# A fused attention and mixture-of-experts kernel: the experts' tokens transposed one tile earlier, and GpSimd's queue reordered

## What is computed

```python
x = x + _L0_xattn_ref(ctx_1024, _layernorm(x), mask, ...)   # perceiver attention, 8 heads of 64, a final layer norm
x = x + _L0_ffn_ref(_layernorm(x), weight_q, weight_scale, bias)   # tokens quantised to int8, one 128x128 product
x = x + _L1_xattn_ref(_layernorm(x), ctx_1024, We, W2)      # attention over 77 context rows, softmax over the tokens
x = x + _L1_ffn_ref(_layernorm(x), Wr, br, W1, b1, W2, b2)  # 8 experts, top 1
# the last one, per token:
expert_idx = argmax(xf @ Wr.T + br)
h = relu(xf @ W1[e].T + b1[e]); y = h @ W2[e].T + b2[e]     # W1 512x128, W2 128x512, e = expert_idx
```

## Time and profile before

| | |
|---|---|
| median of 3 runs | 955.97 us (955.83 to 957.16) |
| the profiled execution | 956.35 us, span 954.6 us from the first to the last instruction |
| TensorE busy | 906.6 us (95%), its granted clock 0.998 of full speed |
| VectorE busy | 745.8 us (78%) |
| ScalarE busy | 693.6 us (73%) |
| GpSimd busy | 459.0 us (48%) |

### The profile page before, as it was taken

The page is one execution under the profiler, slowest core; times in us unless marked ns, Lnnn a source line. Parts: engine busy times, 40 slices in busy tenths (PEclk is TensorE's granted clock), DMA queues, the critical chain, the costliest instruction groups (busy, mean ns, idle before and its releaser), DMA issues.

```text
span 954.6 us, 30726 instructions
## 1 busy us (share of the span) xinstructions
PE 906.6 (95%) x11238; PEld 788.0 (83%) x11238; DVE 745.8 (78%) x2524; ACT 693.6 (73%) x1671; POOL 459.0 (48%) x1094
## 2 busy tenths in 40 slices
PE   3899999999999999999999999999999999899997
PEld 2688888788878887888888888888888878898997
DVE  4666788888878888888888888888888978877553
ACT  2777777777777777777777777777777766676664
POOL 4333333354545444544445454545453544777554
PEclk9999999999999999999999999999999999999999
DMA  6742000000000000000000000000000012245310
GB/s 177 222 131 43 2 2 2 3 13 3 10 5 11 5 8 7 8 8 8 7 8 8 8 8 7 8 8 8 7 8 7 8 41 72 65 96 108 96 52 21
DMA packets 45193, 31.44 MB, mean 33 GB/s; under 512 B 11555, under 2 KB 40166, under 8 KB 45046
## 3 DMA queue, kind: packets, MB, share of 16 engines
q1 hardware_dynamic: 39446, 19.93, 8.8%
q0 software_dynamic: 4320, 8.50, 2.8%
q10 hardware_dynamic: 1280, 1.05, 0.3%
HBM read 17.75 MB, written 12.17 MB: 31 GB/s over the span
## 4 chain that ended last, share of the span: by engine, by line
PE 68%; DVE 15%; ACT 8%; POOL 4%; issue 4%; DMA 0%; DVEq 0%; POOLq 0%; SPq 0%; ACTq 0%
PE ps L1652 9%; PE ps L1605 9%; PE ps L1580 7%; PE ps L1698 6%; PE ps L1396 5%; PE ps L1567 5%; PE ps L1559 5%; PE ps L1398 5%; PE ps L1397 5%; DVE sumsq L1292 4%; PE ps L1657 3%; PE ps L1682 2%; ACT probs L593 2%; ACT qk_hat L606 2%; PE ps L1435 1%
## 5 line engine op out<-in xcount | busy, mean ns | idle before, releaser
L1324 DVE TENSOR_TENSOR qk_hat<-ps,rstd 128x512 f32<-128x512 f32 x168 | 106.4, 685 | 50.1 <-POOL rstd L835 50.1
L1292 DVE TENSOR_REDUCE sumsq<-qk_hat 128x8 f32<-128x512 f32 x168 | 107.8, 678 | 34.6 <-ACT qk_hat L606 33.5
L828 POOL TENSOR_TENSOR rs_t<-rs_y 128x32 f32<-128x32 f32 x73 | 17.5, 240 | 234.7 <-ACT rs_y L647 234.7
L1605 PE MATMUL ps<-v_x,prob 128*64 128x65 f32 x2048 | 127.9, 225 | 2.1 <-ACT w_all L617 0.4
L1605 PE MATMUL ps<-v_c,prob 128*64 128x65 f32 x2048 | 124.3, 222 | 0.0
L1396 PE MATMUL ps<-w_hi,xc_hi 128*128 128x512 f32 x272 | 121.6, 447 | 2.3 <-POOL xc_lo L802 2.3
L666 ACT ACTIVATE prob<-ps,neg_shift 128x512 f32<-128x512 f32 x128 | 88.4, 691 | 48.6 <-PE ps L1652 48.6
L606 ACT ACTIVATE qk_hat<-ps 128x512 f32<-128x512 f32 x168 | 98.7, 599 | 33.5 <-PE ps L1398 27.9
L1605 PEld LDWEIGHTS ps<-v_x,prob 128*64 128x64 f32 x2048 | 105.0, 137 | 20.9 <-issue 19.3
L1652 PE MATMUL ps<-qT_all,kT_all 64*128 64x128 f32 x1536 | 111.6, 285 | 2.9 <-ACT w_all L617 1.2
L1398 PE MATMUL ps<-w_hi,xc_lo 128*128 128x512 f32 x272 | 108.0, 397 | 0.0
(11 more groups left out here) (241 smaller groups left out, 2248.2 us busy)
## 6 DMA issues: line engine op xcount, KB each, us to landing
x_res<-sorted_rows SPq DMA_DIRECT2D x71, 65.5 KB
w_all<-in_L_ffn_W_dram SPq DMA_DIRECT2D x16, 256.0 KB, 5.0
sorted_rows<-fill SPq DMA_DIRECT2D x8, 327.5 KB, 7.4
out_dram<-prob,x_res POOLq DMA_INDIRECT x71, 2.3
sorted_rows<-stage,idx POOLq DMA_INDIRECT x64, 2.4
ctx_res<-in_ctx_dram SPq DMA_DIRECT2D x8, 115.5 KB
x_res<-in_x_dram SPq DMA_DIRECT2D x1, 768.0 KB
sorted_rows<-fill SPq DMA_DIRECT2D x1, 524.0 KB, 4.7
```

What stands on the lines that cost most here:

```text
L1292: nc.vector.reduce_sum(sumsq[:, n * H:(n + 1) * H], sq[:, n * INNER:(n + 1) * INNER].rearrange("p (h d) -> p h d", d=DH), AX).then_inc(ss_ ...
L1324: nc.vector.tensor_tensor(qk_hat[:, n * INNER:(n + 1) * INNER].rearrange("p (h d) -> p h d", d=DH), ps_qk[:, n, :].rearrange("p (h d) -> p ...
L1605: last = nc.tensor.matmul(dst[half:half + DH, :], prob[:, kt, col + half:col + half + DH], v, start=kt == 0, stop=kt == 1)
```

## The change

- `turned(k)` names the tiles transposed in step k: tile 0 in step -1, tiles 1 and 2 in step 0, then tile k+2. TensorE, ScalarE (the copy) and VectorE (`t_now`, in `prep(k)` the tiles of `turned(k+1)`) follow it. TensorE waits before the transpose for the copy of tile n-2, and before the first products also for the relu of tile k-2.
- GpSimd, from round 64 on: variances, root and centred tokens first, then the bias, then two stores, the scatters, one store. The stores are those of one step earlier than before, so each round's last store goes to the next round. The last group's four scatters stand together after all of round 74's stores.
- The second table's four pieces go one to a step (steps 32 to 35), where steps 32 and 33 had two each.

```diff
+        def turned(k):
+            return [n for n in ({-1: [0], 0: [1, 2]}.get(k, [k + 2])) if 0 <= n < T]
 # ScalarE, tile(k)
-                if inside or has_tile(k + 1):
-                    past(act, "T_done", k + 4 * four + 1)
+                for n in [k + 2] if inside else turned(k):
+                    past(act, "T_done", n + 4 * four)
                     if k == -1:
                         act.wait_ge(lo_done, B)
-                    nc.scalar.activation(t_t[:, (k + 1) % 4, :], ps_t[(k + 1) % 2], ACT.Copy).then_inc(se["t_copied"], 1)
+                    nc.scalar.activation(t_t[:, n % 4, :], ps_t[n % 2], ACT.Copy).then_inc(se["t_copied"], 1)
...
-            at, turns = NA, (T - 1 - NA) // 4
+            at, turns = NA, (T - 2 - NA) // 4
 # GpSimd, run(j)
-                if rho == 2 and group(g, inside):
-                    after(pool, "x2_done", g - 1, inside)
-                    ...
-                if rho in (1, 2) and (inside or 0 <= g - 2 < NG - 1):
-                    scatter(g - 2, (2 * rho - 2, 2 * rho - 1), inside)
+                def biased():
+                    if rho == 2 and group(g, inside):
+                        after(pool, "x2_done", g - 1, inside)
+                        ...
+                def scattered():
+                    if rho in (1, 2) and (inside or 0 <= g - 2 < NG - 1):
+                        scatter(g - 2, (2 * rho - 2, 2 * rho - 1), inside)
+                if not tail(j, inside):
+                    biased()
+                    scattered()
...
                 if tail(j, inside):
+                    biased()
+                    store(tile_no(j, 0) - 1)
                     store(tile_no(j, 0))
+                    scattered()
                     store(tile_no(j, 1))
                     if g - 2 == NG - 1 and rho == 0:
                         pool.wait_ge(padded, 16 * E)
-                        scatter(g - 2, (0, 1), inside)
-                    store(tile_no(j, 2))
-                    if g - 2 == NG - 1 and rho == 0:
-                        scatter(g - 2, (2, 3), inside)
+                        scatter(g - 2, (0, 1, 2, 3), inside)
...
             rounds_written_out(run)
+            store(REST[0] - 1)
             for k in REST:
                 store(k)
 # VectorE, prep(k) and the steps after round 74
+                for n in turned(k + 1):
+                    past(dve, "T_done", n - 4)
+                    dve.wait_ge(ld[n % DEEP], 16 * (n // DEEP + 1))
+                    row = rows[:, n, :]
+                    nc.vector.tensor_scalar(t_now[:, n % 4, :], row[:, 0:D], row[:, D:D + 1], row[:, D + 1:D + 2],
+                                            ALU.subtract, ALU.mult).then_inc(se["t_set"], 1)
                 if has_tile(k + 2):
                     n, e = (k + 2) % 4, number[k + 2]
-                    past(dve, "T_done", k - 2)
-                    dve.wait_ge(ld[(k + 2) % DEEP], 16 * ((k + 2) // DEEP + 1))
                     row = rows[:, k + 2, :]
-                    nc.vector.tensor_scalar(t_now[:, n, :], ...).then_inc(se["t_set"], 1)
...
-                if k < REST[2]:
-                    for piece in (0, 1):
-                        last_table(2 * (k - REST[0]) + piece)
+                if k < REST[4]:
+                    last_table(k - REST[0])
                 finish(k)
 # TensorE, tile(k)
-                if has_tile(k + 1):
-                    past(pe, "t_set", k + 1)
-                    if k == 0:
+                for n in turned(k):
+                    past(pe, "t_set", n)
+                    past(pe, "t_copied", n - 2)
+                    if n == 1:
                         pe.wait_ge(exp_done, 4 * B)
-                    nc.tensor.transpose(ps_t[(k + 1) % 2], t_now[:, (k + 1) % 4, :], ident[:, :]).then_inc(se["T_done"], 1)
+                    nc.tensor.transpose(ps_t[n % 2], t_now[:, n % 4, :], ident[:, :]).then_inc(se["T_done"], 1)
                 if has_tile(k):
                     past(pe, "t_copied", k)
+                    past(pe, "relu_done", k - 2)
                     past(pe, "w1_set", k)
```

More of the change, by code:

```diff
@@ L769, in run @@
                     nc.gpsimd.tensor_copy(ctx_now[:, :, :], ctx_res[:, bass.ds(first, 3), :]).then_inc(s["ctx_taken"], 1)
-                if rho == 2 and group(g, inside):
-                    after(pool, "x2_done", g - 1, inside)
[L773 to L776, removed]
-                if rho in (1, 2) and (inside or 0 <= g - 2 < NG - 1):
-                    scatter(g - 2, (2 * rho - 2, 2 * rho - 1), inside)
+                def biased():
+                    if rho == 2 and group(g, inside):
+                        after(pool, "x2_done", g - 1, inside)
+                        pool.wait_ge(x1_done, G * (g + 1))
+                        nc.gpsimd.tensor_tensor(xb[:, :, :], grp(x_res, g),
+                                                bias_b[:, :].unsqueeze(1).to_broadcast([P, G, D]),
+                                                ALU.add).then_inc(s["xb2_done"], 1)
+                def scattered():
[4 more added lines that the diff above has]
+                    scattered()
                 def centred(j, g):
@@ L892, in prep @@
             def prep(k):
+                for n in turned(k + 1):
[4 more added lines that the diff above has]
+                                            ALU.subtract, ALU.mult).then_inc(se["t_set"], 1)
                 if has_tile(k + 2):
                     n, e = (k + 2) % 4, number[k + 2]
-                    past(dve, "T_done", k - 2)
-                    dve.wait_ge(ld[(k + 2) % DEEP], 16 * ((k + 2) // DEEP + 1))
                     row = rows[:, k + 2, :]
-                    nc.vector.tensor_scalar(t_now[:, n, :], row[:, 0:D], row[:, D:D + 1], row[:, D + 1:D + 2],
-                                            ALU.subtract, ALU.mult).then_inc(se["t_set"], 1)
                     past(dve, "relu_done", k - 2)
```

## The result

The changed kernel takes 957.9 us in the median of 14 runs (956.87 to 960.47), the kernel before 955.95 in 14 runs beside it (955.46 to 957.38). The ratio is 1.0021, 95% interval 1.0014 to 1.0028: some 1.95 us slower. The middle of the interval is just over the 0.2% named as the bound, and its lower end under it. The profiled execution took 958.9 us, its span is 957.2, the mean granted clock 0.996 (before 0.998). It is a late one among the 14; the fastest execution of each kernel differs by 1.4 us.

What follows compares the result with a forecast made beforehand. TensorE was taken as the bound, with GpSimd's chain binding from 810.51 to 834.15 us. Start +0.3, bias +0.2, parts 2 to 4 -0.2 sum to +0.3: 956.65 us profiled, 956.3 median, range 953.7 to 958.8.

Steps and rivals of the forecast that it cites:

- rival (b): Tile 41's load, behind fourteen stores and scatters ahead of the last scatter, comes late: 958.4 us; chance 0.17.
- Start, +0.3: Round 64: VectorE prepares tokens 1 and 2 in a row, one more 0.32 us operation TensorE waits for: +0.3 us.
- Waits for copies: TensorE's products no longer wait for ScalarE's token copies; TensorE 1.5 us ahead at round 68, -0.2 us after 840 us.
- The bias beside VectorE, +0.2: Group 14's bias, moved to about 795.2 us, runs beside VectorE's preparing of tile 5: +0.2 us, bounds 0 and 0.8.
- GpSimd's gap: GpSimd idle 2.35 instead of 0.70 us ahead of round 68's root; round 69's variances 1.65 us later, taken as +1.4.
- +0.95 at 839 us: Delay left at 839 us: +1.4 from GpSimd less 0.45, with VectorE's 0.40 us idle ahead of the logits' transpose regained.
- Late next, and no loss by itself: VectorE's sum of round 69, at 829.97 us, would wait for the bias done at 829.0 us, costing nothing by itself.
- Table, -1.5: One second-table piece a tile makes no tokens late and removes TensorE's 1.36 us hole: -1.5 us.
- Loads: Last scatter at 878.7, first load at 881.9 us; tile 41's load is later, so parts 2 to 4 give -0.2, not -0.75.
- rival (c): The table's spread doesn't help because VectorE loses its lead elsewhere; the 1.5 us stay: 957.5 us, chance 0.08.
- (a): Faster: GpSimd opens no gap, its root of 68 finds ScalarE free, or its chain is no bound: 953.8 us, chance 0.22.
- (d): Two-ahead copies don't free TensorE, since the wait on the relu of tile k-2 binds: 956.8 us, chance 0.05.

Runs made afterwards that it cites:

- copies alone: Kernel before with only the copies made two tiles ahead: 955.51 against 955.61 us, ratio 0.9999.
- order alone: Kernel before with only GpSimd's roots and centred tokens moved ahead of bias, stores and scatters: 961.15 against 955.61 us, ratio 1.0053.
- ten buffers: The changed kernel with ten result buffers in place of eight: 957.22 us against 955.61 for the kernel before, ratio 1.0015.
- table alone: Kernel before with only the second table's pieces spread over four tiles: 954.68 against 955.61 us, ratio 0.9988.
- filled: The changed kernel with ten result buffers plus fourteen unread TensorE transposes in round 69: 959.17 against 955.85 us for the kernel before, ratio 1.0036.
- copies and table: Kernel before with copies two tiles ahead and table pieces on four tiles, GpSimd's order unchanged: 955.66 against 955.85 us; slower chip 977.92 against 977.78.
- the change with ten buffers and bias between: Changed kernel, ten result buffers, GpSimd's bias between variances and root: 983.15 against 977.78 us and 984.53 against 977.55 for the kernel before, slower chips.

## Why the prediction was right or wrong

The forecast was 956.3 us, +0.3 us; measured were +1.95, inside the range and at the foot of "slower". The no-change that had the largest chance did not come. That the time lies in the range is in part luck: the range reached up to 958.8 us for the late load of rival (b) and the collision on the bias, and neither of them occurred. The loss came in good part by a step that the sum did not have, the store.

- **Start, +0.3.** Right. Tile 1's group of products in round 64 is late by 0.25 us against the tile 0 transpose ahead of it (785.01 and 785.41, then 795.56 and 795.71), and copies alone ends at 0 net. The two more waits a tile, put at 0, cost nothing that can be seen: the lateness stays at 2.65 us from tile 39 to 902 us.
- **Waits for copies.** Right: none is left. TensorE comes 2.4 us earlier to tile 13's transpose (822.21 against 824.66) and waited for GpSimd instead.
- **The bias beside VectorE, +0.2.** Not seen. The bias ran from 794.64 us for 1.18, VectorE's preparing at 795.70 took 0.32 us as in the earlier trace rows, and its other operations there 0.17 to 0.35. The centring at 825.10 did stretch one addition to 1.12 us. By the lock that the Trainium skill (SBUF — State Buffer, section "SBUF: two separate sides") describes, VectorE is held when it runs in a two-port mode or with two inputs from SBUF. The trace agrees at 825.27 us, where the addition of two SBUF tiles took the 1.12. At 794.64 it doesn't test the rule for such an addition, since that one ran at 796.27 us, after the bias, for 0.29.
- **GpSimd's gap.** The mechanism was right, and the size nearly. The gap of 2.35 us is 2.52 in order alone, and 1.35 in the change, where the variances of round 68 stood only at 822.20 us and the root came at 823.55. The variances of 69 come 1.65 us later by the clock of the trace and 2.0 after taking off that this execution was 0.37 us ahead until 785 us; +1.4 was forecast, +1.9 at the bound.
- **"+0.95 at 839 us".** Too small. The ranks of round 70 start at 840.81 (839.28 before), +1.53, or +1.9 with the 0.37. The 0.45 us that I took off for VectorE's idle time ahead of the logits didn't come back, since the logits' copy on ScalarE stands behind the same root (6.18 us of waiting in place of 2.09). Of it 1.05 is left at 869 us.
- **What I held for no loss.** "Late next, and no loss by itself" was said of VectorE's sum. It is the 1.98 us hole of TensorE at 829 to 831. Time by itself it hardly cost, but it is the hole after which the clock fell in the profiles of the change and of ten buffers.
- **The ring of buffers.** This step is missing. I counted where the stores went on (860.11 to 860.5; it is 860.73), and asked only whether the loads come later, not which result waits for that store's landing. It cost 1.26 us in the row, 1.0 in the experiment. The question "who waits for what is moved" was asked of the scatters and not of the stores.
- **The clock.** Missing as well; nothing in the profile before showed it. In the profiled execution it cost 1.31 us after 874 and some 0.4 before (1.82 less the 1.26 and 0.65 of the hole, of which 0.50 was there before). The median hardly needs it: two of the fourteen executions have a mean clock of 0.999, as profiles without a fall, and took 957.33 and 957.61 us; three at 0.996 took 956.87 to 957.16.
- **Table, -1.5.** -1.59 within the change, between two groups of products; alone it is -0.9. Right for the hole, too large as a gain of the part by itself, since 0.45 us come back behind it.
- **Loads.** Right in the times: last scatter at 878.98 (878.7 forecast). The first load came at 883.97, not 881.9, because the table, finished at 883.2 in the late frame, and not the scatter was last; yet no hole opened at tile 39 or behind it, since TensorE was late itself. The 0.55 us that I took back for the load of tile 41 (-0.2 in place of -0.75) were owed to nothing that the trace shows.

So the sum of the mechanisms had the right sign in most terms, and what made +0.3 into +1.95 is the store (1.0 to 1.3 us) and the larger delay of GpSimd. How much of the rest is the clock's isn't shown; two executions at a mean clock of 0.999 are within 0.6 us of the median.

The 957.5 us of rival (c) are a slip: its own terms (+0.5, +0.95 and -0.2) give 957.2. Of the rivals, (a) fell, GpSimd did open its gap; (b) fell, the time of 957.9 came near its 958.4 but by another way; (c) and (d) fell. The test "variances of 69 near 836 us with ScalarE waiting over 4 us" was met by 835.80 and 6.18.

The best version found is the table alone: 954.68 against 955.61 us, ratio 0.9988 (0.9979 to 0.9997).

## What to carry to other kernels

When work on a queue is moved behind a wait, list all who wait for it, the transfer's landing and the buffers that it frees among them, and not only the engine that is next on the path. Test the parts of a change alone before they are judged together: here one part gave 0.9 us, one nothing, and one took more than both could give. A hole of about two us in TensorE can cost more than its length, so an edit that only shifts idle time isn't neutral, and filling idle time that another engine sets can just move it to the next wait. Where single executions differ by more than the effect, count from a fixed point just ahead of the edit in two profiles, and read the mean clock beside each time.

## What the runs showed of the hardware

**The granted clock falls after some holes and not after others.** Seen with a fall: 1.98 us and 1.26 + 0.65 (the change), 1.96 (ten buffers), 2.08 (filled). Without a fall in the changed part: 1.36 (before), 1.00 (copies), 1.01 (copies and table), and also 1.85 and 2.61 (order alone), where the stretch behind the second stays at 1.00:

```profile
835.00:837.00 2.00, 0.04 (x1) 0.00 (x0) 0.72 (x3) 0.15 (x1) 1.51 (x3) 1.00 0.10 34
...
838.00:841.00 3.00, 3.00 (x30) 3.00 (x29) 1.50 (x8) 2.38 (x11) 2.05 (x6) 1.00 0.00 0
```

So a hole of this length is not enough by itself. Nor is it needed. In copies and table the clock fell at the start of the program behind holes of 1.23 and 0.51 us. The kernel before has the same two holes there and no fall; its rows come first, then those of copies and table (timeline of TensorE, stretches):

```profile
35.64 1.16 PE L1652 MATMUL ps<-qT_all,kT_all 64*128 64x128 f32 x16 [0.51 <-ACT prob L666]
...
36.00:38.00 2.00, 2.00 (x27) 1.74 (x24) 2.00 (x5) 1.64 (x3) 1.92 (x5) 1.00 1.01 316
```

```profile
35.29 1.67 PE L1660 MATMUL ps<-qT_all,kT_all 64*128 64x128 f32 x16 [0.51 <-ACT prob L670]
...
36.00:38.00 2.00, 2.00 (x15) 1.77 (x14) 2.00 (x5) 1.13 (x3) 1.98 (x4) 0.50 1.06 353
```

That fall cost 1.4 us: TensorE was 0.35 us ahead of the kernel before at 35.29 us and 1.08 behind at 39.27. The times of single executions look like chance too. The kernel before has 21 of 29 executions between 955.24 and 955.73 us and eight between 956.48 and 957.30; copies alone eight of eleven below 955.61, the other three 956.6 to 957.0 at clocks of 0.996 and 0.997; the table alone ten of eleven below 954.94; the change is spread over 3.6 us. The Trainium skill (TensorE: Matmul & The Clock Gate, "Part 1: The HAM clock gate") says that the activity is observed by a window that runs freely and doesn't start with the kernel; that agrees with such a spread. That the eight slower executions of before, some 1.3 us above the others, are due to one fall each is likely, since the fall in copies and table cost 1.4 us and their mean clocks of 0.996 and 0.997 are lower too; no profile of one was taken.

**Some chips are 22 us slower in one part of the program.** Up to 785 us the stretches agree within 0.15 us with the other chips (from 100 to 200 us, TensorE's busy time is 97.69 us against 97.67). From there on, where the rounds stand in the code one by one, consumers wait for TensorE's products for several us, and in four of the six profiles TensorE is seen to pause inside a group of eight products, in which nothing waits (the change with ten buffers and bias between, timeline of TensorE, and VectorE next to it):

```profile
874.23 0.61 PE L1581 MATMUL ps<-w_all,kT_all 128*128 x4
875.06 0.70 PE L1581 MATMUL ps<-w_all,kT_all 128*128 x4 [0.22 <-issue]
```

```profile
878.07 0.29 DVE L932 TENSOR_TENSOR prob<-ps,qT_all 128x128 f32<-128x128 f32 x1 [6.30 <-remote]
```

VectorE gets the products of 875 us only at 878; the profile names no engine of this core as the releaser. Rows with this `remote` are in all six profiles of these chips and in none of the other eight. The Trainium skill (Runtime: NRT & Kernel Launch, section "Instruction fetch mechanics") says that an engine's instructions are refilled by a DMA in blocks of 16 KiB and that this is mostly hidden; the profile's instruction queue does carry 92 packets, 1.51 MB together, so 16 KB each, on both kinds of chips. Whether late refills are the cause here wasn't tried, and stays open.

**A store's landing depends on what else is moved.** Indirect stores that land after 2.2 us by themselves took up to 8.4 beside the fills of 327.5 KB, whose own time to landing is 4.7 to 10.3 us there. It differs between profiles with the same fills: the largest that the traces have for a store issued from 855 to 875 us is 5.3 us before, 8.4 in the change and 10.4 in copies and table, where no result waits for it. So the price of the moved store depends on the execution too: order alone has a wait of 0.78 us for it, the change 1.46. The transfer time of a store that frees a buffer has to be read from the stretch where it will stand.
